# A fused attention and feed-forward kernel: differences moved from VectorE to GpSimd, a context product ahead of ten small products, and two banks for the last products

## What is computed

```
x = x + xattn0(layernorm(x), ctx)      # 32 heads of 128, position bias, mask; the layer norm is its own residual
        h_q, h_k, h_v = rms(h) @ w_q.T, ctx @ w_k.T, ctx @ w_v.T
        score = softmax(where(mask, h_q @ h_k.T + position_bias, -inf))
        hidden + (score @ h_v) @ w_out.T
x = x + ffn0(layernorm(x))             # x @ W_base.T + b_base, plus 4 of 16 low-rank experts (rank 8),
                                       # mixed by softmax(log(prior + eps) + x @ router_W.T + router_b)
x = x + xattn1(layernorm(x), ctx)      # softmax((x @ Wq.T + bq) @ (ctx @ Wk.T + bk).T / sqrt(512)) @ ctx
x = x + ffn1(layernorm(x))             # 6-bit codes unpacked, (codes - zero_point) * scale, plus bias
```

## Time and profile before

| | us |
|---|---|
| median of 3 runs | 967.88 |
| lowest and highest run | 967.50, 968.49 |
| profiled execution | 970.49 |
| span in the trace of that execution | 968.7 |
| PE busy in the span | 943.7 |
| DVE, POOL, ACT busy | 636.8, 516.7, 407.9 |

### The profile page before, as it was taken

One profiled execution on the slowest core, in us unless ns is written; L12 is line 12 of the kernel. 1 busy time (PEld: TensorE's weight loads), 2 busy tenths in 40 slices (PEclk: granted clock), 3 DMA queues, 4 the chain that ended last, 5 costly groups with the idle time before them and its releaser, 6 DMA issues.

```text
span 968.7 us, 16920 instructions
## 1 busy us (share of the span) xinstructions
PE 943.7 (97%) x5501; PEld 819.2 (85%) x5501; DVE 636.8 (66%) x1162; ACT 407.9 (42%) x1141; POOL 516.7 (53%) x579
## 2 busy tenths in 40 slices
PE   8999999999999999999999999999999997999996
PEld 7888888888889888988888888888888885777774
DVE  5665765555856685667666766676756678467885
ACT  5654425334343434443443343434334334234553
POOL 3450734476656655675557565756674632032567
PEclk9999999999999999999999999999999997999999
DMA  9224437663667356745683667365736563300001
GB/s 328 101 79 144 141 121 284 199 224 131 250 229 272 131 220 229 277 149 219 222 284 128 243 209 273 117 259 190 280 123 247 193 217 132 118 3 1 33 30 59
DMA packets 61146, 171.70 MB, mean 177 GB/s; under 512 B 6039, under 2 KB 8219, under 8 KB 60844
## 3 DMA queue, kind: packets, MB, share of 16 engines
q1 hardware_dynamic: 61100, 171.11, 50.0%
HBM read 159.56 MB, written 11.53 MB: 177 GB/s over the span
## 4 chain that ended last, share of the span: by engine, by line
PE 87%; DVE 7%; ACT 2%; issue 2%; POOL 1%; DMA 1%; POOLq 0%; SPq 0%; ACTq 0%; DVEq 0%
PE ps_o L347 6%; PE ps_q L347 6%; PE ps_q L349 6%; PE ps_q L348 6%; PE ps_o L349 6%; PE ps_o L348 6%; PE ps_k L347 5%; PE ps_t L2103 5%; PE ps_k L348 5%; PE ps_k L349 5%; PE ps_s L2076 5%; PE ps_v L347 5%; PE ps_v L349 5%; PE ps_v L348 5%; PE ps_t L2093 3%
## 5 line engine op out<-in xcount | busy, mean ns | idle before, releaser
L761 ACT ACTIVATE scores<-scores,neg_max 128x128 f32<-128x128 f32 x256 | 99.8, 391 | 234.9 <-DVE neg_max L1529 234.9
L1416 DVE TENSOR_TENSOR acc<-ps_o,acc 128x512 f32<-128x512 f32 x128 | 87.8, 686 | 64.1 <-PE ps_o L349 64.1
L347 PE MATMUL ps_o<-wo_hi,att_hi 128*128 128x512 f32 x256 | 107.1, 419 | 8.1 <-DVE att_lo L1404 7.4
L349 PE MATMUL ps_o<-wo_hi,att_lo 128*128 128x512 f32 x256 | 101.1, 395 | 0.0
L348 PE MATMUL ps_o<-wo_lo,att_hi 128*128 128x512 f32 x256 | 100.9, 394 | 0.0
L767 ACT COPY probs_t<-ps_t 128x512 f32<-128x512 f32 x64 | 37.6, 588 | 141.8 <-PE ps_t L2093 141.8
L1064 POOL TENSOR_TENSOR shift<-bias_sb,mask_sb 128x512 f32<-128x512 f32 x64 | 84.2, 1315 | 5.6 <-DVE scores L1525 5.6
L1404 DVE TENSOR_TENSOR att_lo<-ps_t,att_hi 128x512 fp32r<-128x512 f32 x64 | 44.2, 691 | 58.3 <-ACT att_hi L754 58.3
L1105 POOL TENSOR_TENSOR wq_lo<-raw_q,wq_hi 128x256 fp32r<-128x256 f32 x65 | 48.5, 746 | 59.9 <-ACT wq_hi L593 59.9
L347 PE MATMUL ps_v<-wv_hi,ct_hi 128*128 128x256 f32 x264 | 75.0, 284 | 0.3 <-POOL wv_lo L1085 0.2
L349 PE MATMUL ps_v<-wv_hi,ct_lo 128*128 128x256 f32 x264 | 74.7, 283 | 0.0
(11 more groups left out here) (375 smaller groups left out, 2774.1 us busy)
## 6 DMA issues: line engine op xcount, KB each, us to landing
ring_hi<-scratch_x_t SPq DMA_DIRECT2D x39, 512.0 KB, 4.1
ring_lo<-scratch_x_t SPq DMA_DIRECT2D x39, 512.0 KB, 4.9
ring_hi<-scratch_c_t SPq DMA_DIRECT2D x39, 512.0 KB, 4.1
ring_lo<-scratch_c_t SPq DMA_DIRECT2D x39, 512.0 KB, 5.4
raw_o<-in_w_o SPq DMA_DIRECT2D x16, 512.0 KB, 4.8
raw_q<-in_w_q SPq DMA_DIRECT2D x15, 512.0 KB, 6.4
raw_k<-in_w_k SPq DMA_DIRECT2D x15, 512.0 KB, 7.2
xt_hi<-scratch_x_t SPq DMA_DIRECT2D x13, 512.0 KB, 7.4
```

The source lines that it names most:

```text
L347: pe.matmul(dst, hi_l, hi_r, start=first, stop=False)
L349: return pe.matmul(dst, lo_l, hi_r, start=False, stop=last)
L761: e = act.activation(probs[n][:, m, :], scores[n][:, m, :], ACT.Exp, bias=neg_max[:, n, m:m + 1], accum_out=row_sum[:, n, m:m + 1])
L1416: dve.tensor_tensor(acc[:, b, :], ps_o[:], acc[:, b, :], ALU.add).then_inc(o_added, 1)
```

## The change

It has eight parts.

1. DVE: the 13 small instructions move from behind step 7 to three places behind steps 2, 3 and 4.
2. POOL: at step 8 `wo_lo` is formed ahead of `wv_lo`.
3. PE: in steps with `c` = 0 of turns 2 to 7, `q_p3(g)` moves ahead of `v_p5(i, 0)`, and so ahead of the transposes.
4. The four `wk1_lo` differences go from DVE to POOL, behind `wo_lo` of group 15 and ahead of a `shift`. ACT makes two of the high parts ahead of `pt_evac(60)` and two behind the cast of `wo_hi`. On DVE `wq1_lo` is spread over step 61: two ahead of the second addition of step 60's output, one behind it, one behind `att_lo` of step 61.
5. PE: in step 61 four matmuls of ones by ones, 128x128, into `ps_v`, whose result nobody reads. In step 62 `product_m(0)` goes ahead of the first part of the output products of step 61, `product_m(1)` between the parts.
6. `spread_kb` writes `ps_q2` and no longer waits for the selection. `product_g(0)` follows it at once, then the ten small products, which no longer wait for the copy of `kb_row`, the second part of the output products of step 62, the transposes of step 63, `product_g(1)`, the low-rank pair, the values.
7. ACT takes the exponentials of step 63 ahead of the logarithm, and DVE the softmax of step 63 and the additions of step 62 ahead of the copies that need it.
8. The end: `c_product` writes `ps_q2` for tiles 0 to 4 and 6 and `ps_k` for 5 and 7, and from tile 5 on it waits for one scaling less. The bias sum of tile 7 goes to a tile of its own, `f_last`, on POOL right behind that of tile 6, ahead of tile 5's shift and finish; on DVE `shift_rest(7)` stands ahead of `c_scale(6)`.

The second shift has moved from behind `finish_rest(6)` to ahead of `c_scale(6)`. The diff, cut to its core:

```diff
+        f_last, _ = place("f_last", [P, D], F32, at=at_wq + 8192 + 6144)
...
+        c_banks = (ps_q2,) * 5 + (ps_k, ps_q2, ps_k)
...
+        wk1_lo_s = mask_done
...ACT
-            pt_evac(STEPS - 4)
-            split_o(GROUPS - 1)
...
+            wk1_high_part(0)
+            wk1_high_part(1)
+            pt_evac(STEPS - 4)
+            split_o(GROUPS - 1)
+            wk1_high_part(2)
+            wk1_high_part(3)
...
-            act.copy(kb_row[:], ps_v[:]).then_inc(kb_s, 1)
+            act.copy(kb_row[:], ps_q2[:]).then_inc(kb_s, 1)
+            exponentials(STEPS - 1, 1)
             act.wait_ge(lr_mm, 1)
             act.activation(logit_bias[:, 0, :], ps_v[:, 148:152], ACT.Ln, bias=prior_eps[:, 0:1]).then_inc(lbias, 1)
-            exponentials(STEPS - 1, 1)
-
+            pt_evac(STEPS - 1)
...POOL
+                if c % 4 == 0:
+                    rest_o(g)
                 if first:
                     rest_v(PLAIN)
-                if c % 4 == 0:
-                    rest_o(g)
+                if last and c == 4:
...
+                        pool.tensor_tensor(wk1_lo[:, m, :], wk1_raw[:, m, :], wk1_hi[:, m, :].bitcast(F32),
+                                           ALU.subtract).then_inc(wk1_lo_s, 1)
...
+                if tc == BATCH - 1:
+                    pool.wait_ge(codes_s, 4)
+                else:
+                    wait_from(pool, c_add, tc - 1)
...DVE
+                if s == 2:
+                    target_experts()
+                if s == 3:
+                    target_rows()
+                if s == 4:
+                    target_copies()
+                    bias_product()
...
+            softmax_front(STEPS - 1, 1)
+            add_output(STEPS - 2, 6, (0,))
+            softmax_back(STEPS - 1, 1)
+            add_output(STEPS - 2, 6, (1,))
             dve.wait_ge(lr_mm, 1)
...
-            step_drain(STEPS - 1, 7)
...PE
                 if last and c == 5:
                     k_p3(g)
+                    pe.wait_ge(v_out, v_count(i, 14))
+                    for _ in range(4):
+                        pe.matmul(ps_v[:, 0:P], ones[:], ones[:], start=True, stop=True)
...
                 if c == 0 and own:
+                    q_p3(g)
                     v_p5(i, 0)
...
+            product_m(0)
             output(s - 1, 5, None, (0,))
-            product_m(0)
+            product_m(1)
             output(s - 1, 5, None, (1,))
-            product_m(1)
...
-                pe.wait_ge(sel_s, 1)
-                pe.matmul(ps_v[:], ones[:], w_rows[:, 1, :], start=True, stop=True).then_inc(kb_mm, 1)
+                pe.wait_ge(mm_out, 3)
+                pe.matmul(ps_q2[:], ones[:], w_rows[:, 1, :], start=True, stop=True).then_inc(kb_mm, 1)
...
-            pe.wait_ge(kb_s, 1)
+            product_g(0)
+            pe.wait_ge(sel_s, 1)
...
-                wait_from(pe, c_scaled, b)
+                wait_from(pe, c_scaled, b if b < 5 else b - 1)
```

114 lines of the change are left out of this document (58 added, 56 removed).

## The result

The changed kernel takes 956.03 us (median of 4 runs, 955.01 to 957.22) against 967.69 us (967.22 to 968.49): a ratio of 0.9879, 95% interval 0.9862 to 0.9896. That is 11.7 us less, where 7.5 were forecast; the time lies near the low end of the range, 955.5 to 964.4. The profiled execution took 957.22 us, with a span of 955.3 us against 968.7.

What follows compares the result with a forecast made beforehand. PE, busy 943.7 of 968.7 us, was taken as the bound, so only its idle time, clock and the last microseconds count. Terms -2.9 - 5.0 + 0.8 - 0.4 = -7.5 gave 960.4 us, range 955.5 to 964.4.

Steps and rivals of the forecast that it cites:

- main part: Steps ahead of the drain: small DVE instructions, `wo_lo` first and `c` = 0 waits together -2.9 us, between -2.0 and -3.4.
- Small DVE instructions, `wo_lo`: Steps 7 and 8: PE's waits for `att_lo` and `wo_lo` go, -0.66 and -0.88 us.
- The `c` = 0 steps: Transposes' waits for DVE's L1538, covered by six matmuls moved ahead: -1.4 us, bounds -1.0 and -2.0.
- Steps 60 and 61: Waits for `att_lo` and half clock shrink, a new wait of step 61's transposes comes: -5.0 us, bounds -7.5 and -3.5.
- even chance of a fall of the clock: Step 61: the new wait of 1 to 3 us may lower the clock again, charged +0.85 us.
- Small products and step 63: `spread_kb` to step 63: DVE's chain becomes the bound and the clock may fall, +0.8 us, bounds -1.0 and +2.0.
- The end: Last tiles: reordered bias sum, shifts and finishes bring the last sum earlier, -0.4 us, bounds 0 and -1.7.
- The sign that was named for it: At the end, DVE's last sum comes 0.2 to 0.8 us earlier against PE's last matmul.
- (a): Rival: the clock holds everywhere; small products -1.0, steps 60 and 61 -5.9, sum -10.2, 957.7 us; chance 0.16.
- (b): Rival: POOL and DVE block each other at every operation, and the clock falls at step 61; 963.2 us; chance 0.12.
- (c): Rival: PE's waits move instead of going; main part -0.7, end nothing; 963.0 us; chance 0.10.
- (d): Rival: the clock falls before step 61's transposes and stays at 1.2 GHz through the weight products; 973 us; chance 0.04.

Runs made afterwards that it cites:

- small_o_back: The changed kernel with the 13 small DVE instructions back behind step 7 and `wv_lo` ahead of `wo_lo` in step 8; 958.41 us, ratio 0.9893.
- q3_back: The changed kernel with `q_p3` of the `c` = 0 steps put back behind the values; 961.81 us, ratio 0.9923.
- after_again: The changed kernel run once more, unchanged, beside the kernel before; 957.29 us, ratio 0.9881.
- all_three: The changed kernel with the `wk1_lo` differences on DVE, step 63's `att_lo` ahead, and tile 5's last sum on DVE; 954.23 us, ratio 0.9856.

## Why the prediction was right, and where it was off

**Direction and range held**; the gain was half as large again as forecast. That the range held owes something to luck: the profiles differ by 13.4 us, 1.0 more than the largest gain that the range allows (12.4, from 967.88 to 955.5), and the medians by 11.7, because the profiled execution of the kernel before lay 2.8 above its median. The main part alone was -5.1 against bounds of -2.0 to -3.4. By its steps:

- *Small DVE instructions, `wo_lo`* (-0.66, -0.88): right, -0.8 and -0.8, and small_o_back brings back both. That the wait called "issue" was `wo_lo`'s is shown.
- *The `c` = 0 steps* (-1.4, bounds -1.0 and -2.0): mis-sized, -3.5, outside its bounds. The term added the idle times that the waits view lists. It left out the 0.16 that the prediction itself had added everywhere else, six times, and the slower transposes behind each stop, about 0.25 six times: 1.4 + 1.0 + 1.6, of which 0.5 came back at step 17. That last wait is in the changed kernel's profile and not in after_again's, so which of the waits occur differs from one execution to the next.
- *Steps 60 and 61* (-5.0): the waits went and came as described, the size was -6.9. PE did start its output products right behind `wo_lo` (0.53 idle), and the new wait for L1558 is there, 1.58 instead of 2.7. Ahead of the transposes of step 61 it gave -3.6 where the term had -2.7. The term put the transposes 6.35 us behind PE's start: the 4.75 of the kernel before, less 0.3 for which it gives no reason, and 1.9 of blocking. Measured were 5.45, of which 1.4 is blocking. The chain of before already had a held-up operation in it, which the term took for unblocked:

```profile
810.12 0.63 DVE L1529 TENSOR_SCALAR neg_max<-row_max 128x4 f32<-128x4 f32 x1
```

  It takes 0.17 in the changed kernel. From the start of L1525 to the end of L1538 it was 4.88 us; less 0.46 for this and plus 1.4 of blocking it is 5.8, as measured. Behind the transposes the gain was -3.3 where the term had -2.35. The even chance of a fall of the clock was charged with 0.85, and no fall came there in the changed kernel's profile; in q3_back it did, and cost 1.3. The wait charged with 0.3 did not come either.
- *Small products and step 63* (+0.8): 0.0. The removed wait (0.7) was replaced by DVE's chain, as said: new waits of 1.2 for `stacked`, and 1.3 for `att_lo` in after_again; in the changed kernel's profile the slow `product_g(2)` hid the second. The fall of the clock right behind the small products was there in 9 of the 11 profiles with the new order, and in the other two it came one product later. The term's sum at full clock was 20.5 from the start of `spread_kb`, 19.5 from its end; from the rows of all_three and after_again it is 19.9, so the sum was 0.6 too long. The fall cost 1.5, where two in three of 2.4 to 2.8 were charged, 1.8, and a second fall, inside the wait, 0.2. 19.9 + 1.5 + 0.2 makes the 21.5 of the changed kernel's profile, where the term had 20.5 + 1.8.
- *The end* (-0.4): -0.8. The blocking is there as forecast (1.47, 1.77, 1.74), `finish_c(5)` (1.53) ended within 0.3 of where the term had it, and the last sum at the early one of the two times it gave, 965.5 (952.89 + 12.54, the shift at the output products of step 63). The sign that was named for it, DVE's last sum 0.2 to 0.8 earlier against PE's last matmul, came out the other way: 4.0 us behind it instead of 3.2, since PE's last matmul came 1.7 earlier, and DVE sets the end.
- *Rivals.* (a), the clock holds, 957.7, gave the time nearest to the measured one. It is right for steps 60 and 61, not for the small products; that it came so near is luck, as the main part, -5.1 for its -2.9, made up for that. (b) and (c) are refuted by the account. (d), a clock that stays low, didn't occur in any of 13 profiles; the longest fall was 7 us.

## What to carry to other kernels

Work that stands ahead of what the busiest engine waits for has to move in its own engine's order first; another engine for it may not be needed, and may cost. A wait on the busiest engine costs more than its listed idle time: compare the starts around it with the same place undisturbed. Before taking a chain of operations from a trace as the unblocked one, look whether one of them was held up there already; an operation moved to another engine may then hold up its former neighbours by running beside them. And a slow stretch in front of a wait is free only as long as the wait is there, so two repairs on one stretch can be worth more, or less, than their sum.
